# Another order of the 16 samples, 40 instead of 12 slots kept in SBUF, and the small weights moved to SyncE's queue

## The chip, the cores and the metric

One core of a Trainium2 chip runs the whole kernel. The metric is the device time of one execution in microseconds (us). The time of the kernel before is the median of three runs; the profile is of one further execution. u stands below for one slot of x: 128 partitions x 4 x 768 float32, 1.573 MB.

## The reference

x is 16 samples of 64 x 64 pixels and 768 channels, float32 (201.3 MB; the result is as large).

```python
xn  = group_norm(x, 32 groups, over pixels and 24 channels)      # per sample
xc  = conv1x1(xn, 768 -> 16) + b1                                # one image of 16 channels
g   = softmax over the two largest of 4 logits, from mean(xc) @ H_w.T + H_b   # [16, 4]
gw  = reshape(g, (4, 16, 1, 1, 1))                               # so sample b's gates come from samples
                                                                 # b//4, 4 + b//4, 8 + b//4, 12 + b//4
mix = sum over e of gw[e] * (resize up by 2**e, conv3x3 (16 -> 16) + bl, resize back)
out = x + conv1x1(mix, 16 -> 768) + b2
```

The reshape ties the samples together: the result of samples 0 to 3 can't be started before samples 0, 4, 8 and 12 have been reduced to their small image; 4 to 7 need 1, 5, 9 and 13; 8 to 11 need 2, 6, 10 and 14; 12 to 15 need 3, 7, 11 and 15. The gates fold the four experts into one 3x3 convolution for each sample with gate-dependent taps, and special taps at the borders.

## The kernel before, in words

**Two passes for each sample.** Pass A of a sample reads its eight slots of x, takes the group statistics (VectorE: 28 of 32 groups, `groups`, L888; ScalarE: the other four, `scalar_group`, L793 and L795), folds them into scaled weights (`fold`, L895 to L920; its last instruction is L918), transposes the slots on TensorE (24 steps of 8 transposes, `transpose`, L644), copies each step to SBUF on ScalarE (L776) and projects it to 16 channels (`project`, L657). Pass B builds the seven tap matrices of a sample (GpSimd, `weigh_taps` and L607), convolves its small image (`conv`, 7 parts, L709), spreads the result (`spread`, L728 and L729, copied by ScalarE at L829), expands it to 768 channels (`tile`, 32 tiles, L740) and adds each tile on VectorE to x in place (`add`, L967). A tile pair, half a slot, is then stored.

**Slots.** x doesn't fit: SBUF holds 13 slots (`SLOTS`), a sample has eight. So x is read twice, once for A and once for B, except for slots that are kept from A to B. `KEPT = {0: 4, 15: 8}` says how many of a sample's slots are kept: 12 in all.

**Orders written out by hand.** Nothing is decided while it runs. `A_ORDER` and `B_ORDER` give the samples' order in the passes. `TRANSFERS` is the order in which SyncE issues every transfer of x: `L4.0:0` loads slot 0 of sample 4 for pass A into place 0, `R0.4.0:6.0` reloads the first half of slot 4 of sample 0 for pass B into half 0 of place 6, `S0.4.0` stores that half. SyncE goes through the list in order. Ahead of a load it waits until the place is free, which is after the transposes of the slot there (L477) or after the landing of the store of the half there (L480); ahead of a store it waits for the half's two adds (L487). While it waits, everything behind waits too. `PE_ORDER`, `ACT_ORDER` and `DVE_ORDER` give in the same way the order of the work on TensorE, ScalarE and VectorE: T and M are a transpose and a projection step, Z and F the sum and the fold of the statistics, G, H and P the gates, C a part of the convolution, X a part of the spreading, E and A a tile and its add, B and S the groups' statistics on VectorE and ScalarE. PSUM has three buffers in turn (`ring_ps`) for T, Z, X, E and G.

**Weights.** ScalarE issues all loads of weights on its own queue ahead of its first work: eight copies each of conv1_w and conv1_b (L753, L754), eight of convl_w (L756), conv2_w (L758), H_b (L760), eight each of convl_b and H_w (L763, L764) and two of conv2_b (L768). GpSimd waits for the late ones ahead of the copy at L570 and `expert_taps`.

Of the kernel before, what the change touches and what calls it, by code (L numbers as in the profile page):

```python
# [13 lines left out]
B, HH, WW, D = 16, 64, 64, 768  # L14
# [23 lines left out]
A_ORDER = [4, 8, 12, 0, 1, 2, 3, 9, 13, 5, 6, 7, 14, 10, 11, 15]  # L38
B_ORDER = [0, 1, 2, 3, 5, 6, 7, 4, 10, 11, 15, 8, 9, 12, 13, 14]
# [3 lines left out]
KEPT = {0: 4, 15: 8}  # L43
# [4 lines left out]
L4.0:0 L4.1:1 L4.2:2 L4.3:3 L4.4:4 L4.5:5 L4.6:6 L4.7:7 L8.0:8 L8.1:9 L8.2:10 L8.3:11 L8.4:12 L8.5:6 L8.6:7 L8.7:4  # L48
L12.0:5 L12.1:2 L12.2:3 L12.3:0 L12.4:1 L12.5:4 L12.6:7 L12.7:6 L0.0:12 L0.1:10 L0.2:11 L0.3:8 L0.4:9 L0.5:6 L0.6:7
L0.7:1 L1.0:4 L1.1:0 L1.2:3 L1.3:2 L1.4:5 L1.5:1 L1.6:7 L1.7:6 L2.0:9 R0.4.0:6.0 R0.4.1:6.1 L2.1:7 L2.2:1 L2.3:5  # L50
S0.0.0 S0.0.1 S0.1.0 S0.1.1 S0.2.0 R0.5.0:12.0 S0.2.1 R0.5.1:12.1 S0.3.0 R0.6.0:10.0 S0.3.1 R0.6.1:10.1 S0.4.0 S0.4.1
L2.4:11 S0.5.0 S0.5.1 L2.5:2 S0.6.0 S0.6.1 L2.6:3 R0.7.0:8.0 R0.7.1:8.1 L2.7:6 R1.0.0:0.0 R1.0.1:0.1 L3.0:4 S0.7.0
L3.1:12 S0.7.1 L3.2:10 S1.0.0 S1.0.1 R1.1.0:8.0 R1.1.1:8.1 R1.2.0:0.0 R1.2.1:0.1 L3.3:3 L3.4:6 S1.1.0 S1.1.1 S1.2.0
S1.2.1 R1.3.0:8.0 L3.5:2 L3.6:11 R1.3.1:8.1 R1.4.0:0.0 R1.4.1:0.1 L3.7:1 S1.3.0 L9.0:5 S1.3.1 S1.4.0 L9.1:7 S1.4.1
R1.5.0:8.0 L9.2:9 R1.5.1:8.1 R1.6.0:0.0 R1.6.1:0.1 S1.5.0 S1.5.1 R1.7.0:8.0 S1.6.0 L9.3:1 L9.4:11 S1.6.1 R1.7.1:8.1
S1.7.0 R2.0.0:0.0 L9.5:2 L9.6:6 R2.0.1:0.1 L9.7:3 S1.7.1 R2.1.0:8.0 S2.0.0 L13.0:10 L13.1:4 S2.0.1 R2.1.1:8.1
R2.2.0:0.0 L13.2:12 S2.1.0 R2.2.1:0.1 S2.1.1 S2.2.0 R2.3.0:8.0 L13.3:3 L13.4:6 R2.3.1:8.1 R2.4.0:0.0 S2.2.1 S2.3.0
L13.5:2 L13.6:11 S2.3.1 R2.4.1:0.1 S2.4.0 R2.5.0:8.0 L13.7:1 L5.0:9 R2.5.1:8.1 L5.1:5 S2.4.1 S2.5.0 R2.6.0:0.0 L5.2:7
S2.5.1 R2.6.1:0.1 R2.7.0:8.0 S2.6.0 R2.7.1:8.1 L5.3:1 L5.4:11 R3.0.0:0.0 S2.6.1 S2.7.0 S2.7.1 L5.5:2 L5.6:6 R3.0.1:0.1
# [265 lines left out]
def program(nc, x, conv1_w, conv1_b, convl_w, convl_b, conv2_w, conv2_b, H_w, H_b, out):  # L325
# [8 lines left out]
    with ctx:  # L334
# [415 lines left out]
        def _(act):  # L750
# [16 lines left out]
            for row in (64, 96):  # L767
                act.dma_start(b2_raw[row:row + 1, :], conv2_b.unsqueeze(0)).then_inc(late_weights_in, 16)  # L768
# [227 lines left out]
```

## Time and profile before

| | |
|---|---|
| median of 3 runs | 1552.23 us (1551.33 to 1552.73) |
| profiled execution: its own time | 1555.05 us |
| its span | 1553.3 us |
| busy: PE, DVE, ACT, POOL | 78%, 66%, 43%, 20% |
| bytes moved | 587.21 MB, a mean of 378 GB/s |
| read from HBM, written | 384.30 MB, 201.33 MB |

PE is TensorE's matmuls, PEld its weight loads, DVE VectorE, ACT ScalarE, POOL GpSimd, SP SyncE; SPq and ACTq are what those engines' sequencers do, here the issuing of transfers. The span runs from the first to the last instruction of the profiled execution. A share of busy time is a mean over stages that differ, so the views by stretch say more than the totals.

### The profile page before, as it was taken

The page shows a single profiled execution, that of the slowest core. Times are in us where ns is not written, and L with a number is a line of the kernel's source. Part 1 is how long each engine was busy: PE and PEld are TensorE (multiplying, and loading weights), DVE is VectorE, ACT ScalarE, POOL GpSimd, SP SyncE. Part 2 cuts the span into 40 slices and gives each one's busy share as a digit, 9 for nine tenths or more (in the row PEclk, how much of TensorE's full clock was granted, in tenths as well). Part 3 has the DMA queues.
Part 4 walks back from the last instruction along what each step waited for, and adds up shares of the span by engine and source line. Part 5 has one row for each costly group of instructions (what it writes and reads, how often), then busy time and mean ns, then how long its engine had stood idle before and what let it go on. Part 6 is the DMA issues. An engine that isn't in the chain of part 4 may idle for free.

```text
span 1553.3 us, 24104 instructions
## 1 busy us (share of the span) xinstructions
PE 1208.5 (78%) x8700; PEld 827.1 (53%) x8700; DVE 1030.2 (66%) x2747; ACT 665.3 (43%) x1549; POOL 312.2 (20%) x381
## 2 busy tenths in 40 slices
PE   0688889959989696879999886989867975857553
PEld 0466666636666464646767564666544643524221
DVE  6778874577777778676787877675544735545443
ACT  0888874446466574737467474534200100010010
POOL 1630007120410000070413102121344241401000
PEclk9899999969999797889999997989777885757555
DMA  9887845999999999999999999999999999999998
GB/s 327 315 305 275 304 155 199 411 409 395 380 410 410 410 409 390 410 345 394 407 408 409 397 400 362 411 415 415 415 415 413 383 405 413 414 412 410 415 413 333
DMA packets 204842, 587.21 MB, mean 378 GB/s; under 512 B 14130, under 2 KB 14130, under 8 KB 204724
## 3 DMA queue, kind: packets, MB, share of 16 engines
q1 hardware_dynamic: 200320, 585.14, 96.0%
q8 instruction: 69, 1.13, 0.3%
q10 hardware_dynamic: 4404, 0.53, 0.3%
q14 instruction: 49, 0.40, 0.1%
HBM read 384.30 MB, written 201.33 MB: 377 GB/s over the span
## 4 chain that ended last, share of the span: by engine, by line
DMA 45%; PE 30%; SPq 9%; DVE 8%; ACT 2%; ACTq 2%; issue 2%; POOL 1%; DVEq 0%
DMA x_sb<-in_x 32%; PE ring_ps L644 13%; DMA out<-x_sb 13%; PE img_ps L657 6%; PE conv_ps L709 6%; DVE x_sb L967 5%; SPq L480 5%; SPq L487 4%; PE ring_ps L740 3%; DVE stats L888 1%; ACT unread_squares L793 1%; ACT unread_copy L795 1%; ACTq L760 1%; ACTq L756 1%; SPq L477 1%
## 5 line engine op out<-in xcount | busy, mean ns | idle before, releaser
L967 DVE TENSOR_TENSOR x_sb<-x_sb,ring_ps 128x768 f32<-128x768 f32 x512 | 463.3, 949 | 319.1 <-DMA x_sb<-in_x 225.1
L888 DVE BATCH_NORM_STATS2 stats<-x_sb 128x6 f32<-128x192 f32 x1792 | 476.0, 344 | 117.5 <-DMA x_sb<-in_x 69.1
L776 ACT COPY xT<-ring_ps 128x1024 f32<-128x1024 f32 x384 | 375.8, 1014 | 263.5 <-PE ring_ps L644 233.2
L644 PE MATMUL ring_ps<-ident,x_sb 128*128 128x128 f32 x3072 | 401.1, 289 | 65.0 <-DMA x_sb<-in_x 41.3
L740 PE MATMUL ring_ps<-w,es 128*128 128x512 f32 (+1 forms) x1024 | 337.5, 446 | 145.2 <-DVE x_sb L967 140.4
L644 PEld LDWEIGHTS ring_ps<-ident,x_sb 128*128 128x128 f32 x3072 | 361.1, 149 | 128.6 <-issue 97.2
L740 PEld LDWEIGHTS ring_ps<-w,es 128*128 128x128 f32 x1024 | 191.1, 232 | 273.5 <-DVE x_sb L967 196.8
L657 PE MATMUL img_ps<-xT,w 128*32 128x256 f32 x3072 | 217.7, 397 | 40.1 <-DVE w L918 34.3
L709 PE MATMUL conv_ps<-xc,band 128*128 128x1 f32 (+8 forms) x1120 | 227.5, 351 | 19.2 <-POOL band L607 10.3
L607 POOL TENSOR_TENSOR band<-taps,masks 128x640 f32<-128x640 f32 (+1 forms) x112 | 133.0, 1202 | 530.9 <-PE conv_ps L709 527.1
L829 ACT CAST es<-ring_ps 64x1024 fp32r<-64x1024 f32 x64 | 63.4, 1004 | 371.9 <-PE ring_ps L729 371.7
L709 PEld LDWEIGHTS conv_ps<-xc,band 128*128 128x128 f32 x1120 | 159.9, 198 | 96.2 <-issue 92.2
L657 PEld LDWEIGHTS img_ps<-xT,w 128*32 128x32 f32 x3072 | 79.2, 111 | 122.2 <-DVE w L918 39.0
L793 ACT ACTIVATE unread_squares<-x_sb 128x192 bf16<-128x192 f32 x256 | 93.5, 365 | 76.4 <-DMA x_sb<-in_x 36.5
L583 POOL TENSOR_SCALAR taps<-experts,gates 128x400 f32<-128x400 f32 x16 | 20.6, 1289 | 413.1 <-DVE bias_es L952 389.1
L795 ACT ACTIVATE unread_copy<-x_sb 128x192 bf16<-128x192 f32 x256 | 89.7, 350 | 0.0
L669 PE MATMUL ring_ps<-stats,ones 128*128 128x192 f32 x128 | 30.7, 379 | 28.0 <-DVE stats L892 21.4
L793 ACT ACTIVATION_READ_ACCUMULATOR unread_squares<-x_sb 128x1 f32 x256 | 48.7, 190 | 0.0
L795 ACT ACTIVATION_READ_ACCUMULATOR unread_copy<-x_sb 128x1 f32 x256 | 48.5, 189 | 0.0
L728 PE MATMUL ring_ps<-es_hi,pick 32*64 32x512 f32 x128 | 33.1, 530 | 13.4 <-DVE x_sb L967 12.0
L585 POOL TENSOR_SCALAR band<-experts,gates 128x400 f32<-128x400 f32 x32 | 41.2, 1286 | 3.1
L669 PEld LDWEIGHTS ring_ps<-stats,ones 128*128 128x128 f32 x128 | 23.5, 218 | 31.8 <-DVE stats L892 23.3
(94 smaller groups left out, 329.9 us busy)
## 6 DMA issues: line engine op xcount, KB each, us to landing
x_sb<-in_x SPq DMA_DIRECT2D x128, 1536.0 KB, 16.0
out<-x_sb SPq DMA_DIRECT2D x256, 768.0 KB, 14.4
x_sb<-in_x SPq DMA_DIRECT2D x232, 768.0 KB, 14.4
w_rep<-in_L_conv_conv_w ACTq DMA_DIRECT2D x8, 48.0 KB, 6.3
bias<-in_L_conv_conv_b ACTq DMA_DIRECT2D x8, 0.1 KB, 6.1
wl_raw<-in_L_conv_convl_w ACTq DMA_DIRECT2D x8, 9.0 KB, 14.3
bias_l<-in_L_conv_convl_b ACTq DMA_DIRECT2D x8, 0.1 KB
gate_w<-in_L_conv_H_w ACTq DMA_DIRECT2D x8, 0.2 KB
```

The lines of the kernel that those rows point to most:

```text
L480: sp.dma_start(x_sb[:, n[0], 2 * n[1]:2 * n[1] + 2], x_v[s, i[0] // 4, i[0] % 4][:, half]).then_inc(loaded[n], 16)
L607: nc.gpsimd.tensor_tensor(band[:, n % BANDS, :, blocks], taps[:, MAT_ROW_TAP[m]].unsqueeze(2).broadcast_to(full), masks[:, MAT_MASK[m], bl ...
L644: last = nc.tensor.transpose(ring_ps[:, buf, q, half * P:(half + 1) * P], slot("L", a, 2 * c + half)[:, q, k * P:(k + 1) * P], ident[:, :])
L657: last = nc.tensor.matmul(img_ps[32 * q:32 * q + 32, 2 * P * (c % 2):2 * P * (c % 2 + 1)], w1[:, AI[a] % 2, k, R * (1 - c // 2):R * (3 - c ...
L709: last = nc.tensor.matmul(conv_v[:, blk_out, col_out], band[:, n % BANDS, ax].rearrange("p h r -> p (h r)"), xc_v[:, XC_PLACE[b], blk_in, ...
L740: last = nc.tensor.matmul(flat_ps[:, buf, part], es4[:, q, (i % 4) * P:(i % 4 + 1) * P], w2[:, part], start=True, stop=True)
L776: nc.scalar.copy(xT[:, at % XT], ring_ps[:, TURN["T", a, n] % RING]).then_inc(xT_copied, 1)
L793: nc.scalar.activation(unread_squares[:, :, :].rearrange("p (s q) c -> p s q c", s=2), group, ACT.Square, accum_out=stats[:, c, g, 0:1]).t ...
L795: nc.scalar.activation(unread_copy[:, :, :].rearrange("p (s q) c -> p s q c", s=2), group, ACT.Identity, scale=1.0 / HALF, accum_out=stats ...
L829: nc.scalar.copy(es4[0:64, 2 * half:2 * half + 2, :], halves_ps[0:64, TURN["X", b, part] % RING]).then_inc(es4_ready, 1)
L888: ins = nc.vector.bn_stats(stats[:, c, g, :], two_slots(n0, n1, g))
L967: nc.vector.tensor_tensor(x_sb[:, n, 2 * half + q % 2, :], x_sb[:, n, 2 * half + q % 2, :], flat_ps[:, TURN["E", b, t] % RING, 0:D], ALU.a ...
```

## The change

`A_ORDER` and `B_ORDER` are other permutations. Sample 13 is now reduced ahead of the first pass B. 40 slots are kept in place of 12, among them all eight of samples 6, 11 and 15. `TRANSFERS`, `PE_ORDER`, `ACT_ORDER` and `DVE_ORDER` are written anew to match; the work in them is the same, but for the 28 reloads of a slot (56 halves) that are gone: 560 transfers in place of 616. `RING`, `SLOTS` and the other sizes stay.

The small weights but two go to SyncE's queue, behind the first 13 loads of x: 8 copies of convl_w, conv2_w, H_b, convl_b in one broadcast load, 8 copies of H_w, 2 of conv2_b, which makes 21 loads. ScalarE issues one broadcast load each for conv1_w and conv1_b.

```diff
-A_ORDER = [4, 8, 12, 0, 1, 2, 3, 9, 13, 5, 6, 7, 14, 10, 11, 15]
-B_ORDER = [0, 1, 2, 3, 5, 6, 7, 4, 10, 11, 15, 8, 9, 12, 13, 14]
+A_ORDER = [12, 9, 4, 8, 0, 13, 2, 1, 3, 5, 6, 10, 7, 14, 11, 15]
+B_ORDER = [0, 2, 1, 3, 5, 6, 4, 7, 9, 11, 10, 8, 12, 14, 13, 15]
-KEPT = {0: 4, 15: 8}
+KEPT = {0: 2, 1: 4, 2: 3, 3: 1, 5: 1, 6: 8, 7: 3, 11: 8, 14: 2, 15: 8}
 TRANSFERS = """
...
+L13.6:7 L13.7:1 L2.0:5 L2.1:2 L2.2:3 L2.3:1 L2.4:7 L2.5:6 L2.6:12 S0.0.0 S0.0.1 S0.1.0 R0.2.0:4.0 S0.1.1 L2.7:10
+L1.0:11 R0.2.1:4.1 R0.3.0:0.0 S0.2.0 R0.3.1:0.1 L1.1:8 L1.2:9 S0.2.1 R0.4.0:4.0 S0.3.0 S0.3.1 R0.4.1:4.1 R0.5.0:0.0
...
+L14.7:7 R4.4.0:1.0 S4.3.1 L11.0:3 R4.4.1:1.1 S4.4.0 R4.5.0:1.0 S4.4.1 R4.5.1:1.1 S4.5.0 S4.5.1 R4.6.0:1.0 R4.6.1:1.1
...
 """
 PE_ORDER = """
...
+M0.20-21 T13.0 M0.22-23 Z13 T13.1 G0 M13.0-1 T13.2-3 M13.2-3 H0 T13.4-7 M13.4-6 T13.8-10 M13.7-9 T13.11-12 C0.0-6
+M13.10-12 T13.13-14 X0.0-1 M13.13 E0.0-1 M13.14 E0.2-7 T13.15-18 M13.15-17 T13.19-21 M13.18 E0.8-9 M13.19-21 T13.22-23
...
 """
-        wl_in = sem("wl_in")
         @block.sync
         def _(sp):
+            def load_late_weights():
+                for h in range(NH):
+                    sp.dma_start(wl_raw[R * h:R * h + R, :, :], convl_w.rearrange("o i y x -> i o (y x)")
+                                 ).then_inc(late_weights_in, 16)
+                sp.dma_start(w2_raw[:, :, :], conv2_w.rearrange("(k c) r y x -> c k (r y x)", k=KB)
+                             ).then_inc(late_weights_in, 16)
+                sp.dma_start(gate_b[0:R, :], H_b.partition_broadcast(R)).then_inc(late_weights_in, 16)
+                sp.dma_start(bias_l[:, :], convl_b.unsqueeze(1).unsqueeze(0).broadcast_to([NH, R, 1])
+                             ).then_inc(late_weights_in, 16)
+                for h in range(NH):
+                    sp.dma_start(gate_w[R * h:R * h + R, :], H_w.rearrange("e r -> r e"),
+                                 allow_slow_non_contiguous=True).then_inc(late_weights_in, 16)
+                sp.wait_ge(bias_zero, 1)
+                for row in (64, 96):
+                    sp.dma_start(b2_raw[row:row + 1, :], conv2_b.unsqueeze(0)).then_inc(late_weights_in, 16)
+
-            for transfer in parse_transfers():
+            for n, transfer in enumerate(parse_transfers()):
+                if n == SLOTS:
+                    load_late_weights()
-            pool.wait_ge(late_weights_in, (4 + 2 * NH) * 16)
+            pool.wait_ge(late_weights_in, (2 * NH + 5) * 16)
-            pool.wait_ge(wl_in, NH * 16)
-                pe.wait_ge(weights_in, 2 * NH * 16)
+                pe.wait_ge(weights_in, 2 * 16)
         @block.scalar
         def _(act):
...
+            act.dma_start(w1_rep[:, :], conv1_w.rearrange("r c y x -> r (c y x)").unsqueeze(0).broadcast_to([NH, R, D])
+                          ).then_inc(weights_in, 16)
+            act.dma_start(bias_1[:, 0:1], conv1_b.unsqueeze(1).unsqueeze(0).broadcast_to([NH, R, 1])
+                          ).then_inc(weights_in, 16)
```

## Rows read from the trace of the kernel before

**Rows 1.** The page: span and data rate in 40 slices.
```profile
span 1553.3 us, 24104 instructions
GB/s 327 315 305 275 304 155 199 411 409 395 380 410 410 410 409 390 410 345 394 407 408 409 397 400 362 411 415 415 415 415 413 383 405 413 414 412 410 415 413 333
```

**Rows 2.** Busy time by stretch: PE, PEld, DVE, ACT, POOL; clock, DMA share, GB/s.
```profile
0.00:10.00 10.00, 0.00 (x0) 0.00 (x0) 2.59 (x16) 0.00 (x0) 6.16 (x23) 1.00 0.83 258
30.00:42.00 12.00, 0.20 (x1) 0.23 (x2) 10.21 (x42) 5.45 (x22) 0.00 (x0) 1.00 1.06 370
59.20:100.10 40.90, 36.95 (x392) 28.11 (x392) 33.24 (x133) 34.61 (x87) 28.11 (x76) 0.96 0.83 310
210.00:220.00 10.00, 10.00 (x119) 7.57 (x113) 6.15 (x24) 9.36 (x24) 0.00 (x0) 1.00 0.03 11
604.40:680.70 76.30, 61.97 (x481) 43.65 (x482) 52.90 (x170) 42.96 (x108) 15.67 (x14) 0.84 1.01 397
680.70:878.00 197.30, 184.15 (x1548) 132.00 (x1548) 151.59 (x455) 117.97 (x284) 51.05 (x50) 0.97 1.01 393
1320.00:1500.00 180.00, 118.11 (x382) 67.27 (x381) 88.83 (x99) 13.81 (x15) 21.73 (x22) 0.61 1.03 413
```

**Rows 3.** SyncE by time: the first loads, the first stores.
```profile
0.81 45.11 SPq L477 DMA_DIRECT2D x_sb<-in_x  x13
236.23 0.88 SPq L480 DMA_DIRECT2D x_sb<-in_x  x2
237.15 22.14 SPq L477 DMA_DIRECT2D x_sb<-in_x  x3
263.17 7.28 SPq L487 DMA_DIRECT2D out<-x_sb  x5
```

**Rows 4.** VectorE by time: end of the folds of samples 4, 1, 2, 15.
```profile
58.93 0.25 DVE L918 TENSOR_TENSOR w<-w1T,of_channel 128x96 f32<-128x96 f32 x1
225.14 0.25 DVE L918 TENSOR_TENSOR w<-w1T,of_channel 128x96 f32<-128x96 f32 x1
343.28 0.25 DVE L918 TENSOR_TENSOR w<-w1T,of_channel 128x96 f32<-128x96 f32 x1
1036.01 0.25 DVE L918 TENSOR_TENSOR w<-w1T,of_channel 128x96 f32<-128x96 f32 x1
```

**Rows 5.** The chain by time, then the timeline; the last row is of the page.
```profile
197.15 2.77 PE ring_ps L644 x24
199.92 1.43 PE img_ps L657 x24
242.98 12.91 PE conv_ps L709 x70
275.16 3.19 PE L740 MATMUL ring_ps<-w,es 128*128 128x512 f32 x8
261.14 14.10 DVE L967 TENSOR_TENSOR x_sb<-x_sb,ring_ps 128x768 f32<-128x768 f32 x16 [3.75 <-PE ring_ps L740]
L829 ACT CAST es<-ring_ps 64x1024 fp32r<-64x1024 f32 x64 | 63.4, 1004 | 371.9 <-PE ring_ps L729 371.7
```

**Rows 6.** Landing times of loads of x; a late chunk's first statistics.
```profile
DMA to landing us min/median/max: 4.3/14.4/25.6
247.64 7.37 DVE L888 BATCH_NORM_STATS2 stats<-x_sb 128x6 f32<-128x192 f32 x28 [14.87 <-DMA x_sb<-in_x]
```

**Rows 7.** The first 50 us by time: small loads, first work.
```profile
9.10 8.47 ACTq L756 DMA_DIRECT2D wl_raw<-in_L_conv_convl_w  x8
18.11 9.33 ACTq L760 DMA_DIRECT2D gate_b<-in_L_conv_H_b  x1
29.10 0.44 ACTq L764 DMA_DIRECT2D gate_w<-in_L_conv_H_w  x1
36.30 1.28 ACT L793 ACT_TABLE_LOAD   x1 [36.30 <-issue]
41.76 7.37 DVE L888 BATCH_NORM_STATS2 stats<-x_sb 128x6 f32<-128x192 f32 x28 [1.14 <-DMA x_sb<-in_x]
```

More of the change, by code:

```diff
@@ new lines @@
+R14.6.1:1.0 R14.7.0:1.1 S14.4.1 S14.5.0 S14.5.1 S14.6.0 S14.6.1 R14.7.1:10.1 S14.7.0 R13.0.0:7.0 R13.0.1:7.1
+R13.1.0:10.0 R13.1.1:1.0 R13.2.0:1.1 S14.7.1 S13.0.0 S13.0.1 S13.1.0 S13.1.1 R13.2.1:10.1 S13.2.0 R13.3.0:7.0
+R13.3.1:7.1 R13.4.0:10.0 R13.4.1:1.0 R13.5.0:1.1 S13.2.1 S13.3.0 S13.3.1 S13.4.0 S13.4.1 R13.5.1:10.1 S13.5.0
+R13.6.0:7.0 R13.6.1:7.1 R13.7.0:10.0 R13.7.1:1.0 S13.5.1 S13.6.0 S13.6.1 S13.7.0 S13.7.1 S15.0.0 S15.0.1 S15.1.0
+S15.1.1 S15.2.0 S15.2.1 S15.3.0 S15.3.1 S15.4.0 S15.4.1 S15.5.0 S15.5.1 S15.6.0 S15.6.1 S15.7.0 S15.7.1
@@ L147 @@
+E14.14-15 X14.3 C15.0-1 E14.16-17 C15.2-6 E14.18-31 X13.0-1 E13.0-13 X13.2 E13.14-15 X13.3 E13.16-31 X15.0-1 E15.0-13
+X15.2 E15.14-15 X15.3 E15.16-31
 """
 ACT_ORDER = """
[L152 to L154 removed]
@@ L750, in _ @@
         def _(act):
-            for h in range(NH):
-                rows = slice(R * h, R * h + R)
-                act.dma_start(w1_rep[rows, :], conv1_w.rearrange("r c y x -> r (c y x)")).then_inc(weights_in, 16)
-                act.dma_start(bias_1[rows, 0:1], conv1_b.unsqueeze(1)).then_inc(weights_in, 16)
-            for h in range(NH):
-                act.dma_start(wl_raw[R * h:R * h + R, :, :], convl_w.rearrange("o i y x -> i o (y x)")
-                              ).then_inc(wl_in, 16)
-            act.dma_start(w2_raw[:, :, :], conv2_w.rearrange("(k c) r y x -> c k (r y x)", k=KB)
-                          ).then_inc(late_weights_in, 16)
-            act.dma_start(gate_b[0:R, :], H_b.partition_broadcast(R)).then_inc(late_weights_in, 16)
-            for h in range(NH):
-                rows = slice(R * h, R * h + R)
-                act.dma_start(bias_l[rows, :], convl_b.unsqueeze(1)).then_inc(late_weights_in, 16)
-                act.dma_start(gate_w[rows, :], H_w.rearrange("e r -> r e"),
-                              allow_slow_non_contiguous=True).then_inc(late_weights_in, 16)
-            act.wait_ge(bias_zero, 1)
-            for row in (64, 96):
-                act.dma_start(b2_raw[row:row + 1, :], conv2_b.unsqueeze(0)).then_inc(late_weights_in, 16)
+            act.dma_start(w1_rep[:, :], conv1_w.rearrange("r c y x -> r (c y x)").unsqueeze(0).broadcast_to([NH, R, D])
+                          ).then_inc(weights_in, 16)
+            act.dma_start(bias_1[:, 0:1], conv1_b.unsqueeze(1).unsqueeze(0).broadcast_to([NH, R, 1])
+                          ).then_inc(weights_in, 16)
             act.wait_ge(consts_ready, 1)
```

249 lines of the change are left out of this document (113 added, 136 removed).

## The prediction

> **What bounds the kernel now.** I read the page's slices first. They move about 300 GB/s while only pass A runs, drop to 155 and 199 where the slots are full and no store has begun, and stay at 380 to 417 from there to the end [rows 1]. Then the busy time by stretch, with three regimes. (1) A alone: 40.9 us for a sample, PE busy 36.95 of them, transfers busy 0.83 of the time; TensorE and the fold's chain set the pace. (2) A and B mixed, as in 680.7 to 878: PE 184 of 197 us and transfers 393 GB/s, so both are near their limits. (3) B alone, as in 1320 to 1500: 413 GB/s, PE at a granted clock of 0.61 with idle time; transfers alone set the pace [rows 2]. From the chunks being stored at 263.2 us to the end, 327 of 372 u are moved in 1290 us: 3.95 us each, against 1.573 MB / 413 GB/s = 3.81 at the full rate [rows 2, 3].
>
> TensorE's units at full clock are: transposing step 2.77/3 = 0.92 us, projecting step 1.43/3 = 0.48, part of a convolution 12.91/7 = 1.84, tile 3.19/4 = 0.80; a part of the spreading I set at 1.0, its copy on ScalarE [rows 5]. 384 steps, 112 parts, 512 tiles, 64 parts and small things make 1236 us, 77 a sample.
>
> **A sum that can be tested.** I cut the run at the folds of the A samples. Between two folds I count in TRANSFERS the u from one sample's last load to the next one's, and in PE_ORDER the units from one Z to the next, and take the larger of 3.81 us x u and the units. For the kernel before:
>
> - Folds of samples 4 to 1: 58.93 to 225.14, four samples in 166.2 us, 41.6 each [rows 4].
> - Fold of 1 to that of 2: 19 u (72) against 96 units: 96.
> - Ten more folds, to sample 15: maxima 64.8, 68.4, 66.7, 62.9, 64.8, 72.4, 63.8, 64.0, 61.0, 80.1, sum 669; measured 1036.0 - 343.3 = 693 [rows 4].
> - The rest: 141 u, 537; measured 517, since loads run ahead of the fold.
>
> Together 225.1 + 96 + 669 + 537 = 1527, where the span is 1553: the sum is 26 us short. What it lacks are the places where gates are made and both streams wait; 604.4 to 680.7 holds one and took 76.3 us against 64.8 [rows 2].
>
> **The change, part by part.**
>
> *28 slots fewer reloaded.* 56 half loads go, 44.0 MB: 344 u in place of 372. At 3.81 to 3.95 us that is 107 to 111 us if transfers set the pace everywhere they are taken from. Nothing else is removed: engines do the same work.
>
> *One more sample ahead of the first store.* 55 u come ahead of S0.0.0, before 45. The store is one A-alone sample later (41.6) and four transposing steps later, 3.3 us: 263.2 + 44.9. Per u the A stage costs 5.2 us where the later stage costs 3.9. This cost is inside the sum below: what A work is moved to the front is missing later.
>
> *The small weights.* ScalarE starts its first statistics at 36.3 us only because it issues loads until then [rows 7]; the loads of x run at 258 and 370 GB/s beside the small ones [rows 2], and the last chunk of the first sample is read at 41.76 [rows 7]. Without them that chunk could be read at about 14.7 + 3 x 7.6 = 37.5 and ScalarE would wait for nothing: the first fold can end up to 8 us sooner. Against that, SyncE issues 21 small loads ahead of the 14th load of x. By ScalarE's rows: 8.47 for convl_w, 9.33 for H_b (a full queue, most likely), 0.44 for each of the rest, about 23 us from about 42 on [rows 7]. The 14th load would wait until about 60 anyway for the transposes of the slot. So the gain is between 8 and -5; I take 5. GpSimd needs the weights only for the copy that TensorE's W follows, and W stands 3 transposes and more into sample 9, near 95 us: that edit costs nothing, unless the small loads land after about 90, when TensorE would stand still for the difference.
> The Trainium skill (DMA: Bandwidth & Descriptors, Anatomy of one DMA, and its Rules for kernel authors) gives each DMA a fixed cost of about 2.0 us and calls anything under 64 KB mostly overhead; 21 x 2.0 = 42 us in front of the 14th load would make the start about 20 us later in place of 5 sooner, and the total 1490. The rows above show the same loads issued 0.44 us apart, so they overlap, and I follow the rows.
>
> *The intervals of the new order*, u x 3.81 against units:
>
> - start to the fold of 13: 225.1 + 41.6 - 5 = 261.7
> - to 2: 10.5 u (40) / 65.7; to 1: 17.5 u (66.7) / 62.9; to 3: 23 u (87.6) / 97.3; to 5: 20 u (76.2) / 58.1; to 6: 14.5 u (55.2) / 52.2; to 10: 35.5 u (135.3) / 145.5; to 7: 16 u (61.0) / 39.2; to 14: 11.5 u (43.8) / 46.3; to 11: 22.5 u (85.7) / 89.9; to 15: 42.5 u (161.9) / 152.1. Sum of maxima 865.7.
> - the rest: 82.5 u, 314.3 (units 250).
>
> Total 261.7 + 865.7 + 314.3 = 1441.7. Add the 26 us that the sum lacked before, since there are the same four makings of gates, and 3 us at the end: the last sample is all in SBUF, its 8 u of stores need 30.5 us, its 32 tiles at VectorE's 14.10/16 = 0.88 each 28 and the spreading 5 [rows 5]. That is a span of 1471; the profiled execution's own time is 1.75 above its span and 2.8 above the median, so 1470 as a median. Intervals can lend to each other through loads issued ahead, which the maxima forbid: counted in bytes alone, first store at 303.1 and 289 u at 3.95, it is 1444. I take 1465, near the first, since in seven of the ten new intervals the two limits lie within 10% of each other, so that neither can catch up much.
>
> *The written order's distances.* In the list I counted what stands between the reload of a half and its store: median 4.0 u before, 3.0 after; between a store and the transfer that reuses its place: 3.5 before, 2.5 after. 4.0 u are 15.2 us, the median landing 14.4 [rows 6]. If a landing always took 14.4, 3.0 u (11.4 us) would no longer cover it. But the shortest landing is 4.3 us, and the three u issued from 236.2 on were in use at 247.6, just 3 x 3.81 later [rows 3, 6]: a landing is mostly the queue ahead of it. A half's own 1.9 us leave 2.4 fixed. So idle time arises where nothing or 0.5 u stands between: 12 places (5 and 7) against 5 before: 5 x 2.4 + 7 x 0.5 = 16 us at most, nothing where TensorE is the later one. Most lie in samples 3 and 4, in intervals that TensorE sets; I take nothing and keep 16 for the range.
>
> **The rivals.**
>
> *Bytes rule (1405 to 1444).* If loads ahead level the intervals fully, 289 u take 3.81 to 3.95: 303.1 + 1101 = 1404 to 1444. For it: B alone holds 413 GB/s. Against: 393 where TensorE was near its limit [rows 2], and a lower stock of slots free to run ahead. 0.2.
>
> *TensorE and short reload chains rule (1490 to 1540).* Pass B of sample 4 reloads its slots through one place, sample 0 through two, the others mostly through three. The mixed stretch 680.7 to 878, where both limits met, ran 5% under 413 GB/s; 5% of all ten intervals (866) is 43 us, and with the 26, the 3 and the 16 above it makes 1441.7 + 88 = 1530. For it: seven intervals of that kind. Against: the ten folds before took only 3.6% more than their maxima (693 against 669) with the same kind of gates in them. 0.23.
>
> *The order doesn't keep transfers ahead: slower.* Place: every reloaded half behind a store. If a landing keeps near 14.4 us whatever is queued, each store of a reloaded half is issued 3.8 us later than the list allows (15.2 - 11.4). 176 halves with six in rotation are 29 turns: 29 x 3.8 = 110 us, 1465 + 110 = 1575. It decides from 87 / 29 = 3.0 us a turn. Against it stand the 4.3 us and the three u above. 0.06; a result within 0.2% would need it to hit 87 us by chance: 0.01.
>
> **How the numbers follow.** The forecast (1444 to 1490) has 0.5. 0.2% (3 us) is about what a measurement of this kernel can tell from no change. Faster than that: 0.5 + 0.2 + 0.23 = 0.93; same 0.01; slower 0.06. The range leaves out the lower part of the first rival and the upper part of the second: 1422 to 1525.
>
> **What would show it.** The page of the kernel after: 543 MB moved; first store near 303 us; the mean rate from there to the last load near 391 GB/s. TensorE busy over 83% of the span, with a clock above 0.9 up to 1150 us or so. ScalarE's first statistics near 15 us and the first fold near 54: if that fold stands at 59 or later, the small weights' step was wrong. If the rate is 410 all along, bytes rule; if waits of SyncE for a store's landing exceed those for VectorE and the slices fall under 370 with TensorE idle, the short chains do. The fold of 15 should stand near 1150 us and the rest take 314 or a little less. The forecast is wrong if the span lies outside 1440 to 1490.

## The result, and the profile after

The changed kernel took 1489.77 us (median of 4 runs, 1487.68 to 1497.98) beside 1551.78 for the kernel before on the same chip (4 runs, 1550.88 to 1552.73): a ratio of 0.9618, interval 0.9584 to 0.9652. The ratio takes in two more runs (1497.86 and 1492.30 us); by it the saving is 59 us, known to 5. By the medians it is 62 us where 87 were forecast. It lies inside the range (1422 to 1525), and at the upper edge of the forecast's own one (1444 to 1490).

The profiled execution is the longest of the four: 1497.98 us, span 1496.2. Readings of the whole time from this one trace therefore carry some 8 us of scatter.

The page of the kernel after; the second row answers to [rows 1], the last two give KB for each transfer and the median us from issue to landing [rows 6]:

```profile
span 1496.2 us, 24054 instructions
PE 1197.6 (80%) x8700; PEld 834.0 (56%) x8700; DVE 1036.9 (69%) x2747; ACT 665.7 (44%) x1549; POOL 313.9 (21%) x381
GB/s 342 255 335 307 306 306 317 170 291 393 359 366 409 405 413 296 381 401 387 355 376 411 397 362 282 402 408 343 412 372 404 377 397 391 397 408 413 406 402 367
DMA packets 189250, 543.16 MB, mean 363 GB/s; under 512 B 12874, under 2 KB 12874, under 8 KB 189132
out<-x_sb SPq DMA_DIRECT2D x256, 768.0 KB, 10.8
x_sb<-in_x SPq DMA_DIRECT2D x176, 768.0 KB, 11.4
```

543 MB are moved, as said. Behind the slice of the first store and ahead of the last one, ten slices are under 380 GB/s, down to 296 and 282. [rows 1] had two, 345 and 362 (the prediction's "380 to 417" passes over them). Landings are shorter, 10.8 us for stores and 11.4 for half loads against 14.4 for both before: less is queued ahead of each.

Busy time by stretch, columns as in [rows 2], for the kernel after: from the first store to the end, then the stretch in which A and B are mixed.

```profile
307.90:1496.20 1188.30, 963.42 (x6390) 656.84 (x6390) 796.12 (x1815) 443.54 (x959) 240.16 (x232) 0.83 0.99 383
308.00:1183.00 875.00, 726.01 (x5293) 510.44 (x5294) 625.74 (x1599) 394.81 (x905) 173.63 (x168) 0.87 0.98 379
```

The same two for the kernel before:

```profile
263.20:1553.30 1290.10, 1016.00 (x6822) 681.25 (x6822) 839.80 (x2005) 487.05 (x1084) 241.15 (x232) 0.82 1.01 401
308.00:1183.00 875.00, 736.26 (x5732) 516.18 (x5731) 620.67 (x1739) 443.25 (x1024) 166.82 (x161) 0.89 1.02 401
```

289 u in 1188.3 us are 4.11 us each; before, it was 327 in 1290.1, 3.95 each. The 0.17 us more on each of 289 u is 48 us given back. Most of it was in the forecast, whose 1471 - 303.1 = 1168 us for 289 u are 4.04 each; the other 0.07 each, 20 us, were not. TensorE is busy for 726 of 875 us against 736, so it isn't busier either.

SyncE by time in the kernel after: the loads and the small weights, then the first stores [rows 3].

```profile
0.81 43.98 SPq L481 DMA_DIRECT2D x_sb<-in_x  x13
44.83 16.27 SPq L452 DMA_DIRECT2D wl_raw<-in_L_conv_convl_w  x8
...
68.20 219.13 SPq L481 DMA_DIRECT2D x_sb<-in_x  x42
307.93 3.83 SPq L491 DMA_DIRECT2D out<-x_sb  x3
```

VectorE by time: the folds of 12, 9, 13, 2, 10 and 15 [rows 4], and between the first two the statistics of a chunk of the second sample.

```profile
54.40 0.25 DVE L909 TENSOR_TENSOR w<-w1T,of_channel 128x96 f32<-128x96 f32 x1
76.38 7.37 DVE L879 BATCH_NORM_STATS2 stats<-x_sb 128x6 f32<-128x192 f32 x28 [6.50 <-DMA x_sb<-in_x]
100.56 0.25 DVE L909 TENSOR_TENSOR w<-w1T,of_channel 128x96 f32<-128x96 f32 x1
268.28 0.25 DVE L909 TENSOR_TENSOR w<-w1T,of_channel 128x96 f32<-128x96 f32 x1
344.98 0.25 DVE L909 TENSOR_TENSOR w<-w1T,of_channel 128x96 f32<-128x96 f32 x1
...
812.73 0.25 DVE L909 TENSOR_TENSOR w<-w1T,of_channel 128x96 f32<-128x96 f32 x1
1185.53 0.25 DVE L909 TENSOR_TENSOR w<-w1T,of_channel 128x96 f32<-128x96 f32 x1
```

Against the forecast's span of 1471: the start ends at 268.3 in place of 261.7 (+6.6); the ten intervals take 917.2 in place of 865.7 + 26 (+25.5); the rest takes 310.7 in place of 314.3 + 3 (-6.6). That makes 25 us, and the ten intervals hold all of it; that the start and the rest cancel is luck. A second trace of the same orders (e2, span 1489.1) has 913.6 for the ten intervals and 305.3 for the rest, so the first number is good to some 4 us.

**Against the kernel before, interval by interval.** The 26 us that the prediction added is what the kernel before took over its sum of maxima in all. It is the difference of two larger numbers. From the last fold ahead of the first store to the fold of 15, that kernel took 1036.0 - 225.1 = 810.9 us against maxima of 96 + 669 = 765, 46 more; its rest took 20 less (517 against 537) [rows 4]. The same stretch of the kernel after takes 917.2 against 865.7, 51.5 more. That is 6.0% before and 5.9% after. The rest, which has 82.5 u in place of 141, gives back only 3.6 (310.7 against 314.3). What has changed is where the excess lies. The interval with the first store had 22 us of it before (118.1 against 96) and has 11 after (344.98 - 268.28 = 76.7 against 65.7); the others had 24 in 669, 3.6%, and have 40.5 in 800, 5.1%.

**Where in them.** I cut both kernels into windows of 10 us from 310 to 1480 and counted in each what a rate under 413 GB/s loses (10 us x (1 - rate/413)). The kernel before loses 29 us, the kernel after 81. Windows under 330 GB/s hold 14 of the 29 (five windows) and 45 of the 81 (twelve). So 31 of the 52 us more are lost in a few holes. (Not all of the 52 is more than forecast: where TensorE's units exceed the bytes, the maxima have such time in them.) Five of the twelve:

```profile
410.00:420.00 10.00, 7.02 (x31) 3.88 (x31) 9.08 (x22) 0.23 (x1) 0.30 (x1) 0.66 0.73 268
580.00:590.00 10.00, 5.47 (x24) 4.22 (x28) 8.04 (x28) 7.04 (x31) 0.00 (x0) 0.80 0.48 190
590.00:600.00 10.00, 10.00 (x92) 7.47 (x85) 7.45 (x24) 6.17 (x15) 0.00 (x0) 0.85 0.61 167
900.00:910.00 10.00, 10.00 (x77) 7.16 (x76) 7.66 (x24) 6.01 (x11) 1.14 (x1) 1.00 0.82 258
910.00:920.00 10.00, 10.00 (x60) 7.64 (x58) 5.47 (x18) 0.23 (x1) 3.90 (x6) 1.00 0.72 212
```

The DMA share falls to 0.48: half of the time the transfer engines have nothing to do. SyncE's timeline in the hole at 580, then in the one at 900, where sample 4 goes through one place:

```profile
561.95 11.31 SPq L481 DMA_DIRECT2D x_sb<-in_x  x3
583.73 0.38 SPq L491 DMA_DIRECT2D out<-x_sb  x1
590.37 0.37 SPq L484 DMA_DIRECT2D x_sb<-in_x  x1
```

```profile
900.24 0.37 SPq L484 DMA_DIRECT2D x_sb<-in_x  x1
900.65 0.47 SPq L491 DMA_DIRECT2D out<-x_sb  x1
908.72 0.37 SPq L484 DMA_DIRECT2D x_sb<-in_x  x1
909.13 0.47 SPq L491 DMA_DIRECT2D out<-x_sb  x1
916.09 0.37 SPq L484 DMA_DIRECT2D x_sb<-in_x  x1
```

From 573.3 to 583.7 SyncE waits for the first additions of sample 3, then until 590.4 for the landing of that half, whose place the next transfer needs, then once more, until 598.5. In 25 us it issues two half stores and one half load. At 900 there are two such turns, a store and the load into its place 7 to 8 us later.

What SyncE waits for in all, in the kernel after (waiter, released by: us in total, times, the longest):

```profile
SPq L491 <- DVE x_sb L958: 404.7, 189, 20.6
SPq L484 <- DMA out<-x_sb: 300.5, 124, 8.2
```

And in the kernel before:

```profile
SPq L487 <- DVE x_sb L967: 291.7, 152, 6.4
SPq L480 <- DMA out<-x_sb: 171.5, 68, 9.2
```

A load that waits for the store before it to land went from 171.5 us (68 times) to 300.5 (124 times), a store that waits for VectorE's addition from 291.7 to 404.7. The longest such wait, 20.6 us, is the one ahead of the very first store, from 287.3 to 307.9, and no hole; from there on the longest is 11.9 us, where the kernel before had 6.4, and the sum is 384.1. SyncE issues all transfers in one written order, so whatever it waits for holds back what follows. Most of these waits cost nothing, since other transfers are queued: both kinds together grew by over 200 us, and the loss of rate is 48. The share of 0.48 shows a place where too little was queued.

### The profile page after: what moved, and what is told of

Its sections match the earlier page's. It is cut to its first block, busy times and chain, and to the rows that moved or that the text cites. A ratio compares the mean times of both kernels' runs of the same rounds, so it can differ in the third digit from the quotient of the medians.

```text
span 1496.2 us, 24054 instructions
## 1 busy us (share of the span) xinstructions
PE 1197.6 (80%) x8700; PEld 834.0 (56%) x8700; DVE 1036.9 (69%) x2747; ACT 665.7 (44%) x1549; POOL 313.9 (21%) x381
## 4 chain that ended last, share of the span: by engine, by line
PE 47%; DMA 27%; DVE 14%; ACT 4%; SPq 4%; issue 3%; DVEq 0%; ACTq 0%
PE ring_ps L649 19%; DMA x_sb<-in_x 18%; PE img_ps L662 10%; DMA out<-x_sb 9%; PE conv_ps L714 9%; DVE x_sb L958 9%; PE ring_ps L745 7%; DVE stats L879 2%; SPq L481 2%; ACT xT L767 1%; SPq L484 1%; ACT unread_squares L784 1%; PE ring_ps L674 1%; ACT unread_copy L786 1%; SPq L491 1%
## 5 line engine op out<-in xcount | busy, mean ns | idle before, releaser
L745 PE MATMUL ring_ps<-w,es 128*128 128x512 f32 (+1 forms) x1024 | 332.0, 447 | 100.6 <-DVE x_sb L958 86.8
L662 PE MATMUL img_ps<-xT,w 128*32 128x256 f32 x3072 | 216.0, 401 | 54.9 <-DVE w L909 50.7
L714 PE MATMUL conv_ps<-xc,band 128*128 128x1 f32 (+8 forms) x1120 | 221.4, 346 | 6.0 <-ACT xc L794 3.4
L588 POOL TENSOR_SCALAR taps<-experts,gates 128x400 f32<-128x400 f32 x16 | 20.6, 1287 | 431.4 <-DVE bias_es L943 397.2
L808 ACT ACTIVATE es_hi<-conv_ps,bias_es 128x512 fp32r<-128x512 f32 x16 | 11.0, 688 | 121.8 <-PE conv_ps L714 106.2
L733 PE MATMUL ring_ps<-es_hi,pick 32*64 32x512 f32 x128 | 31.9, 531 | 25.5 <-DVE x_sb L958 16.1
## 6 DMA issues: line engine op xcount, KB each, us to landing
out<-x_sb SPq DMA_DIRECT2D x256, 768.0 KB, 10.8
x_sb<-in_x SPq DMA_DIRECT2D x176, 768.0 KB, 11.4
```

Of the source, the lines that this page charges most:

```text
L662: last = nc.tensor.matmul(img_ps[32 * q:32 * q + 32, 2 * P * (c % 2):2 * P * (c % 2 + 1)], w1[:, AI[a] % 2, k, R * (1 - c // 2):R * (3 - c ...
L714: last = nc.tensor.matmul(conv_v[:, blk_out, col_out], band[:, n % BANDS, ax].rearrange("p h r -> p (h r)"), xc_v[:, XC_PLACE[b], blk_in, ...
L745: last = nc.tensor.matmul(flat_ps[:, buf, part], es4[:, q, (i % 4) * P:(i % 4 + 1) * P], w2[:, part], start=True, stop=True)
```

## The experiments

Every change in us below is the difference of two ratios times 1551.8. Since the kernel after is known to 5 us (its interval), a difference under 5 or 6 us says nothing.

**e1. The small weights alone, in the old orders.** The old `A_ORDER`, `B_ORDER`, `KEPT` and written orders with the new loads of weights.

```diff
-            for transfer in parse_transfers():
+            for n, transfer in enumerate(parse_transfers()):
+                if n == SLOTS:
+                    load_late_weights()
```

> The orders and kept slots of the kernel before, with only the small weights moved as in the change. Theory 1 (the 21 small loads on SyncE's queue hold up the 14th load of x and give back what ScalarE's early start brings): the first fold near 54 us in place of 58.9, the second near 100 as before, and the time within 2 us of before (1550 to 1553). Theory 2 (prediction: 5 us gained in all): 1547. Theory 3 (2.0 us for each small load in front of the 14th): about 1570.

Measured: 1554.55 us (12 runs), before 1551.73 (17 runs); ratio 1.0012, interval 1.0000 to 1.0023. Nothing, or up to 3.6 us lost. In its trace SyncE's 14th load of x, and then VectorE's first fold, its reading of the second sample, and the second fold:

```profile
66.79 43.60 SPq L492 DMA_DIRECT2D x_sb<-in_x  x10
```

```profile
54.12 0.25 DVE L920 TENSOR_TENSOR w<-w1T,of_channel 128x96 f32<-128x96 f32 x1
74.99 7.37 DVE L890 BATCH_NORM_STATS2 stats<-x_sb 128x6 f32<-128x192 f32 x28 [5.38 <-DMA x_sb<-in_x]
101.80 0.25 DVE L920 TENSOR_TENSOR w<-w1T,of_channel 128x96 f32<-128x96 f32 x1
```

The first fold is 4.8 us sooner (54.1 against 58.93), but the second stands at 101.8, where the kernel before had it at 99.8: the 14th load is issued at 66.8, hardly later than the 65.5 of the kernel before, but no sooner either, and VectorE waits 5.4 us for its data. What the first sample won, the second lost.

**e2. The orders alone,** with the weights loaded as before (the other half of e1's edit).

```diff
-                if n == SLOTS:
-                    load_late_weights()
...
-                pe.wait_ge(weights_in, 2 * 16)
+                pe.wait_ge(weights_in, 2 * NH * 16)
```

> The new orders and the 40 kept slots, with the small weights loaded by ScalarE at the start as before. Theory 1 (all of the gain is the orders'; the move of the weights is worth nothing net): 1488 to 1492, the first fold near 59 and the second near 100. Theory 2 (the move brings 5): 1495.

Measured: 1494.46 us, ratio 0.9624, 0.9606 to 0.9642, within the interval of the kernel after. The orders with the kept slots are the whole gain. (Its 1494.5 is near the 1495 that stood for "the move brings 5", but by the ratios it is 1 us above the kernel after, with 5 of error.)

**e3. The small weights on GpSimd's queue.** The kernel after, with `load_late_weights` issued by GpSimd, once the third chunk's statistics are taken.

```diff
+            def load_late_weights():
+                pool.wait_ge(stats_taken, 3)
...
+            load_late_weights()
```

> The kernel after, with the 21 late small loads issued by GpSimd, which is idle then, once three chunks of statistics are taken. Theory 1 (SyncE's queue held the start up): the first fold near 54, the second near 95 to 96, and 4 us less at the end, 1486. Theory 2 (the start's gain is lost later, in waits that depend on other things): within 1 us of the kernel after, 1489 to 1491.

Measured: 1493.05 us (6 runs), ratio 0.9606, 0.9576 to 0.9637. The 14th load of x leaves at 61.4 us in place of 68.2, and the folds stand at 54.9, 97.4 and 264.8 (sample 13), so 3.5 us of the start are won against the kernel after. At the end they can't be told from nothing.

**e4, e11, e12. Less work for the engines.** In the kernel after, the convolution with its centre column alone; the statistics over one slot of two; both.

```diff
-                for ax in (MID, LEFT, RIGHT, LEFT_EDGE, RIGHT_EDGE):
+                for ax in (MID,):
```

```diff
-                ins = nc.vector.bn_stats(stats[:, c, g, :], two_slots(n0, n1, g))
+                ins = nc.vector.bn_stats(stats[:, c, g, :], x_sb[:, min(n0, n1), :, g * CG:(g + 1) * CG])
```

> The kernel after with only the centre of the five column taps in each part of the convolution (112 x 4 groups of matmuls left out, so the result lacks the side taps). TensorE's units fall from 1236 to about 1080. Theory 1 (the mixed stage is set by whichever of TensorE and the transfers is larger in each interval): the maxima fall by 35 us, so 1455. Theory 2 (the excess over the maxima comes from TensorE arriving late at the stores, so it shrinks too): 1435. Theory 3 (short reload chains and the order of the list set the pace, not TensorE): no more than 10 us less, 1480 to 1490.

> The kernel after in which VectorE's group statistics read one of a chunk's two slots (half of the elements, so the normalization is of half the data). It takes some 180 us of VectorE's work away. Theory D (adds come late because they stand behind blocks of statistics in VectorE's order, and late adds hold up SyncE's stores): 25 to 50 us less, 1440 to 1465. Theory C (places and latencies, not the engines): under 12 less, 1478 to 1490. A-alone samples should stay near 41 us, since TensorE sets them.

> Both cuts together: statistics of one slot of two, and only the centre column tap in each part of the convolution. Theory D (either engine alone hides what the other's cut would give): far more than the sum of the two cuts, 1420 to 1445, with the mixed stage at 400 GB/s or more. Theory C: about the sum of the two, 1465 to 1480, and the mixed stage stays under 390 GB/s.

Measured: e4 1480.42 us, ratio 0.9541, 0.9520 to 0.9562, some 12 us less than the kernel after (with 6 of error); e11 1494.62, 0.9623, 0.9601 to 0.9645, no effect; e12 1478.66, 0.9532, 0.9486 to 0.9578, the same as e4. Over the whole run e4 takes 106 us of busy time from TensorE, less than the 156 expected. The mixed stretch in e4, e11 and e12, one after the other:

```profile
308.00:1183.00 875.00, 669.67 (x4723) 454.29 (x4722) 636.00 (x1623) 398.16 (x909) 170.08 (x166) 0.81 0.99 385
```

```profile
308.00:1183.00 875.00, 730.67 (x5327) 510.37 (x5326) 533.78 (x1617) 397.62 (x909) 172.59 (x167) 0.88 0.99 383
```

```profile
308.00:1183.00 875.00, 670.89 (x4727) 454.22 (x4729) 530.23 (x1618) 398.69 (x911) 170.56 (x166) 0.81 0.99 384
```

With TensorE busy 56 us less (e4), VectorE 92 us less (e11), or both (e12), the rate is 383 to 385 GB/s in place of 379 and stays far from the 401 of the kernel before. The holes stay as well. The one at 410 comes a window earlier in e4 (258 GB/s from 400 on). At 580 and 900:

```profile
580.00:590.00 10.00, 7.20 (x60) 4.95 (x64) 7.23 (x29) 6.97 (x24) 0.00 (x0) 0.83 0.55 171
590.00:600.00 10.00, 9.99 (x109) 7.83 (x102) 9.69 (x30) 5.58 (x6) 0.00 (x0) 1.00 0.80 267
900.00:910.00 10.00, 6.01 (x27) 4.39 (x26) 7.03 (x20) 0.23 (x1) 4.96 (x6) 0.86 0.59 174
910.00:920.00 10.00, 8.28 (x75) 5.71 (x74) 2.48 (x3) 4.23 (x5) 0.00 (x0) 0.80 0.79 232
```

From 900 to 920 the kernel after had TensorE busy for 20 of 20 us, which reads as if TensorE set the pace there. In e4 it is busy for 14.3 of them, and the rate is no better. (e4 is some 10 us ahead there, so these windows are neighbours of the others rather than the same work.) From 310 to its last transfers, windows under 330 GB/s still lose 36 us in e4 against 45, all windows 63 against 81; these 18 us are nearly the 19 by which the two profiled executions differ. In the hole at 580, SyncE makes the same turns: a store at 577.0, the load behind it at 584.3, the next at 591.5. So most of the holes aren't made by TensorE's work, but a part of the excess is: the ten intervals take 14 us less.

**e5, e6. One sample reloaded again.** `KEPT` of sample 15, of sample 6, from 8 to 0, and its 16 half loads written into `TRANSFERS` ahead of their stores (13 to 25 transfers ahead in e5, 9 to 15 in e6).

```diff
-KEPT = {0: 2, 1: 4, 2: 3, 3: 1, 5: 1, 6: 8, 7: 3, 11: 8, 14: 2, 15: 8}
+KEPT = {0: 2, 1: 4, 2: 3, 3: 1, 5: 1, 6: 0, 7: 3, 11: 8, 14: 2, 15: 8}
```

> The kernel after with the eight kept slots of sample 15 loaded again, each half into its own place some 12 transfers ahead of its store (8 u more, no place is needed). Theory A (the last stage is set by the bytes): 8 x 3.81 = 30 us more, 1520. If TensorE and the adds set the end instead: 5 to 15 more.

> The same for sample 6, in the mixed stage: 8 u more between the folds of 5 and 10. By the maxima of the prediction only what exceeds TensorE's units counts: 20 us more, 1510. If bytes count one for one there too: 30 more, 1520. If the queue has idle time to give in that stage: under 15 more.

Measured: e5 1527.42 us, ratio 0.9851, 0.9829 to 0.9872: 36 us for 8 u. e6 1520.65, 0.9798, 0.9782 to 0.9814: 28 us for 8 u. Those are 4.5 and 3.5 us a u, each with 0.8 of error, around the 3.81 of a stage that transfers set, and not around nothing. In e6 the whole of it lies between the folds of 6 and 10, an interval that the prediction had TensorE set (135.3 against 145.5):

```profile
656.52 0.25 DVE L911 TENSOR_TENSOR w<-w1T,of_channel 128x96 f32<-128x96 f32 x1
840.83 0.25 DVE L911 TENSOR_TENSOR w<-w1T,of_channel 128x96 f32<-128x96 f32 x1
```

It takes 184.3 us in place of 155.6 (657.2 to 812.7). If TensorE had set it, the first 10 us of transfers would have been free and the cost 20.

**e7. Reloads of one tile in place of two.** The kernel after with half the bytes in each of the 176 half loads, 44 u fewer.

```diff
-                    half = slice(2 * i[1], 2 * i[1] + 2)
+                    half = slice(2 * i[1], 2 * i[1] + 1)
```

> The kernel after in which each of the 176 half reloads fetches only the first of its two tiles (44 u fewer; the second tile's result is wrong). Theory A (the time from the first store on is bytes at the full rate plus idle time that stays as it is): 44 x 3.81 = 168 us less where transfers set the pace, bounded by TensorE's units in the intervals: by the maxima 92 less, 1398. Theory C (the pace of the mixed stage is set by the few places in turn, each with a store's and a load's latency and two waits for adds, so that bytes matter only in part): 40 to 70 less, 1420 to 1450.

Measured: 1424.54 us, ratio 0.9182, 0.9167 to 0.9197: 68 us less than the kernel after, 1.5 us for each u. Bytes added cost their full price (e5, e6), bytes taken away below the present number give 40% of it. The total fits Theory C, but not its place. In e7's trace the ten intervals take 878.8 us, 38 less than in the kernel after for 26.5 u fewer, where the maxima allow 28. The rest, after the fold of 15, takes 273.8, 37 less for 17.5 u fewer, where the maxima allow 64: what is missing from the 92 is missing in the last stage, and not in the mixed one. SyncE then waits for VectorE's additions above all:

```profile
SPq L491 <- DVE x_sb L958: 605.5, 244, 20.6
SPq L481 <- PE ring_ps L649: 246.0, 61, 23.8
```

**e9. Close places moved apart.** Six swaps of neighbours (the expectation counts five) at places of the kernel after where a transfer reuses a half close behind the store that frees it. Of the twelve places with at most 0.5 u between, six are left, and none with nothing between. One of them:

```diff
-L14.7:7 R4.4.0:1.0 S4.3.1 L11.0:3 R4.4.1:1.1 S4.4.0 R4.5.0:1.0 S4.4.1 R4.5.1:1.1 S4.5.0 S4.5.1 R4.6.0:1.0 R4.6.1:1.1
+L14.7:7 R4.4.0:1.0 S4.3.1 L11.0:3 R4.4.1:1.1 S4.4.0 S4.4.1 R4.5.0:1.0 R4.5.1:1.1 S4.5.0 S4.5.1 R4.6.0:1.0 R4.6.1:1.1
```

> The kernel after with only TRANSFERS edited in five places where a reload stands right behind the store that frees its place (samples 0 to 4 and the loads of sample 10): the next store or load is put between them. Nothing else moves. Theory A (the time lost in the mixed stage is the transfer queue running dry at such places, about 4 us each, of which this takes away some five): 12 to 20 us less than the kernel after, 1470 to 1478. Theory B (the queue runs dry because adds come late, and those places only fill the time): within 4 us of the kernel after, 1486 to 1494.

Measured: 1498.68 us (5 runs), ratio 0.9658, 0.9636 to 0.9679: no gain, 6 us more if anything, so Theory A fails (and the time lies above Theory B's range too). The waiting changed its name, not its size:

```profile
SPq L491 <- DVE x_sb L958: 440.8, 191, 20.6
SPq L484 <- DMA out<-x_sb: 265.0, 117, 7.3
```

35 us less behind landings, 36 more behind additions; windows under 330 GB/s lose 48 us in place of 45. Where a sample passes through one place, issuing its second store sooner only means waiting for the second addition sooner.

**e10. Close places made.** Near the end, where transfers alone set the pace, 16 half reloads of sample 12 stand each right behind the store that frees their place.

```diff
-R8.6.1:10.1 S8.5.1 R8.7.0:7.0 S8.6.0 R8.7.1:7.1 R12.0.0:10.0 R12.0.1:1.0 S8.6.1 R12.1.0:1.1 S8.7.0 S8.7.1 R12.1.1:10.1
+R12.0.0:10.0 R8.6.1:10.1 S8.5.1 R12.0.1:1.0 R8.7.0:7.0 S8.6.0 R12.1.0:1.1 R8.7.1:7.1 S8.6.1 R12.1.1:10.1 S8.7.0
```

> The kernel after with the 16 half reloads of sample 12, in the late stage that transfers set, each put right behind the store that frees its place. Theory A (about 4 us of idle transfer queue each: the landing of the store, then the start of the load): 16 x 4 = 64 us more, 1554. By the 2.4 us of the prediction: 1528. Theory B (such places cost nothing, other transfers fill them): 1488 to 1495.

Measured: 1548.52 us (10 runs), ratio 0.9986, 0.9971 to 1.0000: 57 us more than the kernel after, 3.6 us for each place; its trace has all of it behind the fold of 15 (367 us in place of 310.7). The same window in e10 and in the kernel after:

```profile
1300.00:1400.00 100.00, 61.26 (x239) 39.40 (x238) 35.86 (x41) 4.65 (x6) 33.29 (x32) 0.67 0.74 234
```

```profile
1300.00:1400.00 100.00, 73.60 (x301) 44.86 (x300) 48.40 (x56) 8.20 (x9) 33.20 (x32) 0.75 1.03 410
```

234 GB/s in place of 410. Moving sixteen transfers by a few positions in a list costs nearly all that the whole change had won. In its trace each turn takes 7 to 9 us (loads at 1304.0, 1311.2, 1320.1, 1327.4) for one half load and one half store, 1 u, where the full rate takes 3.81.

**e13. All stores issued by GpSimd** (from e3), interleaved with its building of the tap matrices; SyncE issues loads alone.

```diff
-                sp.wait_ge(added, BI[s] * TILES + i[0] * QN + 2 * i[1] + 2)
-                sp.dma_start(out_v[s, i[0] // 4, i[0] % 4][:, 2 * i[1]:2 * i[1] + 2],
+                pool.wait_ge(added, BI[s] * TILES + t * QN + 2 * h + 2)
+                nc.gpsimd.dma_start(out_v[s, t // 4, t % 4][:, 2 * h:2 * h + 2],
```

> The kernel after with the late small loads and all 256 stores issued by GpSimd, which follows TensorE's order (a tap matrix for each part of a convolution, a store for each pair of tiles), while SyncE issues only the loads, in the order of the list. A load still waits for the store that frees its place; but a store no longer waits behind such a load, nor a load of a free place behind a store whose adds are late. Theory H (SyncE's single order holds transfers up that could go; the places would suffice): the rate from the first store on rises from about 383 to 395 to 400 GB/s, 1440 to 1460. Theory C (the places in turn and the latencies of a store and a load set the pace): within 10 us of the kernel after, 1480 to 1500. If GpSimd can't issue stores fast enough between its tap matrices, slower than 1500.

Measured: 1535.82 us (6 runs), ratio 0.9907, 0.9888 to 0.9926: 45 us more than the kernel after. SyncE's and GpSimd's largest waits:

```profile
SPq L468 <- DMA out<-x_sb: 726.3, 156, 26.8
...
POOL out L614 <- DVE x_sb L970: 604.5, 163, 21.0
```

This was meant to tell whether the single order of loads and stores on SyncE makes the holes. It doesn't, since GpSimd's list has its own single order, of stores and tap matrices: it waits 604.5 us for additions. The run shows that these two orders together are worse, and leaves the question open. That GpSimd issues too slowly, the condition under which more than 1500 was expected, isn't shown either.

## Why the prediction was right, and where 25 us went

- **28 slots fewer.** Right: with the orders that make it possible, the whole gain (e2). The price of a u was right where bytes are added: 4.5 and 3.5 us against 3.81 to 3.95 (e5, e6). The 107 to 111 us, less a loss at the start and in the intervals, were the right terms.
- **One more sample ahead of the first store.** Forecast 303.1, measured 307.9. The 4.8 us are the next point's.
- **The small weights: gain taken 5, bounds 8 and -5.** Mis-sized. The first fold is where it was said (54.4; said near 54), and ScalarE's first statistics wait for nothing but their data. The step that failed is the weighing of "the 14th load would wait until about 60 anyway" against 23 us of issuing "from about 42 on". Both times were nearly right (61.4 in e3, without small loads on SyncE; 23.3 us from 44.8), but what followed, a 14th load at 68.2, was taken as next to harmless, and it wasn't. (Of them, the eight loads of convl_w took 16.3 us in place of ScalarE's 8.47 [rows 7], the one of H_b 1.34 in place of 9.33.) The next chunk's statistics waited 6.5 us for their data, and the second fold is no earlier. Gain 0 in e1 (between 0 and 3.6 us lost), and the start term of the sum 6.6 us too low. About half of the 6.6 is not the weights': with the new orders and the old weights the fold of 13 stands at 270.3 (e2), 3.6 past the 266.7 of the sum without the gain of 5.
- **The Trainium skill's fixed cost** (DMA: Bandwidth & Descriptors, Anatomy of one DMA). That page of the Trainium skill fits its 2.0 us to DMAs issued from GpSimd and puts most of it down to the confirmation that the last byte has landed; it doesn't say that queued loads add it up, as the prediction's reckoning by it did. Added up, 42 us would have stood ahead of the 14th load. The trace has 23.3 us for the 21, and e1 has no 20 us loss. The total of that reckoning, 1490, is what was measured, but by luck: the time is lost elsewhere.
- **Ten intervals at the larger of two limits: 865.7, with 26 for the gates.** This is the mis-sized term: 917.2 against 891.7. The 26 were a net: 46 us over the maxima up to the fold of 15, less 20 gained in a rest of 141 u. The prediction compared only ten of those eleven intervals ("3.6%") and carried the net over to an order whose rest is shorter and gave back 3.6. With 46 in place of 26 the span comes to 1491, against 1496.2 and 1489.1 in the two traces. So 20 of the 25 us are in both kernels, and the new order adds some 5 (2 by e2's trace). Within that it is better by 11 us around the first store and worse by 16 in the nine intervals behind (40.5 in place of 24; their greater length alone would give 5 of the 16); for these I had written a reason down and given it no time: a lower stock of free slots to run ahead with. That the 26 were "the places where gates are made" was never tested. The rate from the first store on was forecast at 391 GB/s and is 383.
- **Close places: 12, at 2.4 us, taken as nothing, 16 kept for the range.** The price was low: e10 has 3.6 us where nothing hides it. Halving their number gave nothing (e9), so I can't book the time on them one by one.
- **The rest.** 310.7 against 314.3 + 3: right, at nearly the full rate: 410 GB/s in the window from 1300 to 1400, 395 over the whole of it.
- **The signs that were named.** Mass, first fold and rest as said; fold of 15 at 1185 in place of 1150; TensorE 80% busy in place of over 83; granted clock in the mixed stretch 0.87 in place of above 0.9 (before it was 0.89; e4, with less for TensorE to do, has 0.81 and is faster, so the lower clock goes with idle time and is no sign of a TensorE that sets the pace). The profiled span, 1496.2, is outside the 1440 to 1490 that I had set; another run's was 1485.9.

**The rivals.** "Bytes rule" fails at 383 GB/s, and at e7's 1.5 us a u. "The order doesn't keep transfers ahead" at 1575 fails, though its kind of wait is the one that grew most (171.5 to 300.5 us): the loss of rate is far smaller, so most of it lies under transfers still queued. Of "TensorE and short reload chains", TensorE has at most a part: 56 us less of its busy time in the mixed stretch gave 12 us (e4), where the sum of maxima with shorter convolutions gave some 35, and VectorE's share gave none (e11, e12). By this count short reload chains can hold at most what is new in the intervals behind the first store, some 8 to 16 us of the rival's 43.

**What stays open.** That the 28 kept slots more, which leave fewer places in rotation, make the holes, is argued from shorter landings (14.4 to 10.8 and 11.4), from waits and from the place of the holes, not shown: the number of places was not varied, and no run has the new orders with fewer slots kept, but for e5 and e6, whose reloads take no place from others. What the 6% over the maxima is made of, in either kernel, is open too. Whether loads and stores in two independent orders would close the holes wasn't shown either, e13 being confounded.

## What to carry to other kernels

Count bytes, but count next to them what a kept buffer takes from the transfers that could run ahead: here 28 reloads fewer were worth 110 us by their bytes, 87 in the forecast and 62 on the chip, and bytes put back cost 3.5 to 4.5 us a u while further ones removed gave 1.5. A sum of the larger of two limits by interval came out 6% too low here, in both orders. If you calibrate it on the kernel before, do so stage by stage: a net over all stages hid 20 us that one stage lost and another gained. And look at the rate in windows of 10 us, since slices of 37 hide a hole of 190 GB/s. Small loads that are moved from one queue to another move the wait with them: look at which data comes next in the queue that they enter.

## What the runs showed that I had not expected

- A half sent out and its place reloaded right behind it: the load is issued 7 to 8 us after the store (900.65 to 908.72), and sixteen of them in a row cost 3.6 us of transfer time each (e10).
- Eight loads of 9 KB took 16.3 us to issue on SyncE's queue behind 13 large loads, 8.47 on ScalarE's beside them [rows 7].
- A stretch with TensorE busy for all of 20 us at a granted clock of 1.00 moved no faster with a part of TensorE's work left out (e4).
- On the same chip the kernel after scatters over 0.7% in four runs and the kernel before over 0.1%. The latter is in part luck: 17 runs of it beside e1 to e4 scatter over 0.5%.
